# Layer-2 self-attention: the own block's mask enters the scores on TensorE instead of VectorE

## The chip, the cores and the metric

The kernel runs on one core of a Trainium2 chip. The metric is the device time of one execution in microseconds. A core has five engines that run their own instruction queues and meet at semaphores: TensorE (PE; its weight loads are listed as PEld), VectorE (DVE), ScalarE (ACT), GpSimd (POOL) and SyncE (SP), which here only issues DMAs. TensorE writes its products into PSUM, eight banks of 512 float32 columns on 128 partitions; VectorE and ScalarE read them there.

## The reference

The program is a decoder of four layers on x of shape (4, 512, 256) in float32. The change touches one of its twelve parts, the self-attention of layer 2:

```python
q = (x @ Wq.T + bq).reshape(B, T, H, D)      # B 4, T 512, H 16 heads, D 16
k = (x @ Wk.T + bk).reshape(B, T, H, D)
v = (x @ Wv.T + bv).reshape(B, T, H, D)
scores = jnp.einsum('bqhd,bkhd->bhqk', q, k) * attn_scale[0]
mask = _chunk_mask(T, CHUNK)                 # chunks of 64
scores = jnp.where(mask[None, None], -jnp.inf, scores)
attn = jax.nn.softmax(scores, axis=-1)
out = jnp.einsum('bhqk,bkhd->bqhd', attn, v).reshape(B, T, C)
return out @ Wo.T + bo
```

A query sees all keys of later chunks, none of earlier ones, and in its own chunk the keys up to itself. In tiles of 128 queries this means: the key tile of the same index (the own block) is partly masked, later tiles are whole, earlier ones drop out. The input of this part is the layer norm of the running x, and its result is added to x.

## The kernel before, in words

Each part of the model is a stage with its own block of five engine programs; a barrier stands between stages. `l2_attn` (from line 1691) is this stage. Its programs are unrolled lists in a fixed order, with waits on semaphores written out by hand; there is no planner.

**Items.** For each of 4 batches and each of 4 head groups (4 heads of 32 padded rows each, so that the four heads lie on the four 32-row strips of TensorE) there are 4 query tiles of 128: 64 items. An item has two score products. `score` (L1886) makes the scores with queries on the partitions, 128 x 512, 384, 256 or 128 key columns per head, only so that their row maximum can be taken. `row_max` on VectorE adds the mask to the own block, in PSUM, two heads at a time (L2101), and takes the negative maximum over each row, two heads at a time (L2105). When all four tiles of a group are through, the maxima are turned (unit "max") and added to the queries (L2075). `score_T` (L1899), seven items later, makes the scores again with the keys on the partitions, the maximum already in them; ScalarE takes the exponential (L1962), GpSimd cuts the masked part to zero (L2008, L2011), and `attend` (L1913) multiplies with the values and with a column of ones that gives the sums.

**Slots.** All engines walk through the same 79 slots. In slot n TensorE does `score(n)`, the units of `between(n)` (a key projection, a value projection, a turn of x, or the output product of the batch before), in every fourth slot `attend`, then `score_T(n - 7)`, and the units of `behind(n)` (a query projection, turning the maxima, picking and spreading the sums). Within a group the tiles come in the order 0, 3, 2, 1, so the scores have 512, 128, 256 and 384 columns per head.

**Banks.** The two score products share six banks, three pairs in turn (`pair_banks`); banks 6 and 7 serve the units. An item's four heads take two pairs. `pair_emptied` lets TensorE write a pair only after its last reader is done: VectorE's maximum (`maxed`) for `score`, ScalarE's exponential (`exped`) for `score_T`. In a slot, `score_T` needs the pair that the first maximum of that slot's `score` reads, and the next `score` needs the pair of the second maximum and that of the first exponential. `scored` is raised once per item, by the last of its four products.

**Loads.** SyncE loads the padded key and query weights first (`keys_loaded`), then mask, value weights, row vectors, the matrix that picks the sums, and the output weights (`loaded`). TensorE waits for `loaded` after the second score; VectorE waits for it before its first item. The mask is a 128 x 128 tile of 0 and -1e30. `k.ident`, the identity, is in place from the start of the program.

Of the kernel before, what the change touches and what calls it, by code (L numbers as in the profile page):

```python
# [16 lines left out]
ALU = mybir.AluOpType  # L17
# [3 lines left out]
P = 128  # L21
# [10 lines left out]
@contextmanager  # L32
def signals(nc, *names):

    with ExitStack() as st:
        sems = [st.enter_context(nc.semaphore(n)) for n in names]
        yield sems
        nums = sorted(s.num for s in sems)
        for n in nums:
            if n - 1 not in nums:  # L40
                last = n
                while last + 1 in nums:
                    last += 1
                nc.gpsimd.sem_clear(range(n, last + 1))
        nc.all_engine_barrier()
# [1645 lines left out]
def l2_attn(k):  # L1691
    nc = k.nc
    GR, HG, W = 4, 4, 512
# [6 lines left out]
    with ExitStack() as st:  # L1700
        wk, wq, wv, wo = (k.weight(n, st) for n in ("L2_padded_Wk", "L2_padded_Wq", "L2_attn_Wv", "L2_padded_Wo"))
        block_mask = k.const("block_mask", st)
# [19 lines left out]
        ps = k.ps  # L1722
# [40 lines left out]
        def score_op(n):  # L1763
            return n + max(0, n - AHEAD)
# [12 lines left out]
        def pair_banks(o, j):  # L1777
            first = 2 * ((2 * o + j) % 3)
            return slice(first, first + 2)

        with signals(nc, "keys_loaded", "loaded", "ones_set", "stats", "aggr", "shift", "rstd", "normed", "x_turned",
                     "x_moved", "k_projected", "k_made", "q_projected", "q_made", "v_projected", "v_half", "v_made") as (
                keys_loaded, loaded, ones_set, stats, aggr, shift, rstd, normed, x_turned, x_moved, k_projected, k_made,
                q_projected, q_made, v_projected, v_half, v_made), signals(
                nc, "scored", "masked", "maxed", "max_turned", "max_added", "scored_T", "exped", "cut_late", "cut",
                "attended", "summed_out", "picked_out", "inverse_copied", "spread_out", "inverted", "shared", "biased", "out_made", "out_added") as (
                scored, masked, maxed, max_turned, max_added, scored_T, exped, cut_late, cut, attended, sums_copied,
                sums_picked, inverse_copied, sums_spread, inverted, shared, biased, out_made, out_added), nc.Block() as block:

            @block.sync  # L1790
# [7 lines left out]
            LOADS = 16 * (4 + len(k.stage_rows))  # L1798

            @block.tensor  # L1800
            def _(pe):

                def unit(kind, b, i, bank):
                    if kind == "turn":
                        pe.wait_ge(normed, TT * (b + 1))
                        for t in range(TT):
                            last = pe.transpose(ps[:, bank, t * P:(t + 1) * P], xr[:, t, i * P:(i + 1) * P],
                                                k.ident[:, :])
                        last.then_inc(x_turned, 1)
                    elif kind in ("key", "query"):  # L1810
                        pe.wait_ge(x_moved, KC * (b + 1))
                        w = wk if kind == "key" else wq
                        for c in range(KC):
                            last = pe.matmul(ps[:, bank, :], w[:, c, i * P:(i + 1) * P], xT[:, c, :], start=c == 0,
                                             stop=c == KC - 1)
                        last.then_inc(k_projected if kind == "key" else q_projected, 1)
                    elif kind == "value":
                        for t in (2 * i, 2 * i + 1):
                            for c in range(KC):
                                last = pe.matmul(ps[:, bank, t % 2 * D:(t % 2 + 1) * D], xT[:, c, t * P:(t + 1) * P],  # L1820
                                                 wv[:, c, :], start=c == 0, stop=c == KC - 1)
                        last.then_inc(v_projected, 1)
                    elif kind == "max":
                        pe.wait_ge(maxed, 8 * i + 8)
                        for t in range(TT):
                            last = pe.transpose(ps[:, bank, t * P:(t + 1) * P],
                                                top[:, t, i % GR * P:(i % GR + 1) * P], k.ident[:, :])
                        last.then_inc(max_turned, 1)
                    elif kind == "pick":
                        pe.wait_ge(sums_copied, i + 1)  # L1830
                        for t in range(TT):
                            last = pe.matmul(ps[:, bank, HG * t:HG * t + HG], ou[:, i % 2, t * P:(t + 1) * P], sum_rows,
                                             start=True, stop=True)
                        last.then_inc(sums_picked, 1)
                    elif kind == "spread":
                        pe.wait_ge(inverse_copied, i + 1)
                        for t in range(TT):
                            last = pe.transpose(ps[:, bank, t * P:(t + 1) * P], wide[:, t * P:(t + 1) * P],
                                                k.ident[:, :])
                        last.then_inc(sums_spread, 1)  # L1840
                    else:
                        pe.wait_ge(shared, GR * (b + 1))
                        for t in (2 * i, 2 * i + 1):
                            for g in range(GR):
                                last = pe.matmul(ps[:, bank, t % 2 * D:(t % 2 + 1) * D],
                                                 oT[:, b % 2, g, t * P:(t + 1) * P], wo[:, g, :], start=g == 0,
                                                 stop=g == GR - 1)
                        last.then_inc(out_made, 1)
# [28 lines left out]
                def score(n):  # L1877
                    b, g, t, o = n // PER, n % PER // TT, TILE[n % TT], score_op(n)
                    if n % TT == 0:
                        pe.wait_ge(k_made, GR * b + g + 1)  # L1880
                        pe.wait_ge(q_made, GR * b + g + 1)
                    for j in range(2):
                        pair_emptied(o, j)
                    for h in range(HG):
                        r = slice(32 * h, 32 * h + 32)
                        last = pe.matmul(ps[:, pair_banks(o, h // 2).start + h % 2, 0:T - t * P],  # L1886
                                         qT[r, b % 2, g, t * P:(t + 1) * P], kT[r, b % 2, g, t * P:T], start=True,
                                         stop=True)
                    last.then_inc(scored, 1)

                def score_T(m):
# [30 lines left out]
                pe.wait_ge(keys_loaded, 32)  # L1922
                unit("key", 0, 0, 5)
                unit("query", 0, 0, 4)
                for n in range(SLOTS):
                    if n < ITEMS:
                        score(n)
                    if n == 1:
                        pe.wait_ge(loaded, LOADS)
                    for kind, b, i, bank in between(n):  # L1930
                        emptied(*before[bank])
                        unit(kind, b, i, bank)
                        before[bank] = (kind, b, i)
                    if attend_at(n) is not None:
                        emptied(*before[6])
                        attend(attend_at(n))
                        before[6] = ("attend", 0, attend_at(n))
                    if score_T_at(n) is not None:
                        score_T(score_T_at(n))
                    for kind, b, i, bank in behind(n):  # L1940
                        emptied(*before[bank])
                        unit(kind, b, i, bank)
                        before[bank] = (kind, b, i)
# [87 lines left out]
            def _(dve):  # L2031
# [62 lines left out]
                def row_max(n):  # L2094
                    b, g, t, o = n // PER, n % PER // TT, TILE[n % TT], score_op(n)
                    dve.wait_ge(scored, n + 1)
                    if b and n % TT == 0:
                        dve.wait_ge(max_turned, GR * (b - 1) + g + 1)
                    for j in range(2):
                        banks = pair_banks(o, j)  # L2100
                        dve.tensor_tensor(ps[:, banks, 0:P], ps[:, banks, 0:P],  # L2101
                                          block_mask[:, :].unsqueeze(1).to_broadcast([P, 2, P]),
                                          ALU.add).then_inc(masked, 1)
                        dve.wait_ge(masked, 2 * n + j + 1)
                        dve.tensor_reduce(  # L2105
                            top[:, t, g * P:(g + 1) * P].rearrange("p (h d) -> p h d", d=32)[
                                :, 2 * j:2 * j + 2, 16:17],
                            ps[:, banks, 0:T - t * P], AX.X, ALU.max, negate=True).then_inc(maxed, 1)
# [2861 lines left out]
```

## Time and profile before

| | |
|---|---|
| three timed runs | 3913.72, 3920.9, 3924.44 us; median 3920.9 |
| the profiled execution | 3895.01 us, span 3893.3 us |
| TensorE, share of the span | 89% |
| VectorE | 56% |
| ScalarE | 39% |
| GpSimd | 36% |
| mean granted TensorE clock | 0.932 of full |
| layer-2 self-attention | first score at 1586.53 us, last output product ends at 1944.51 us |

The page gives busy time per engine; an engine that is not busy waits for another, and what ended each wait is named behind the arrow in a row. Busy shares over the whole span mix twelve stages, so the rows below look at the one stage. A granted clock of 1.00 stands for 2.4 GHz and 0.50 for 1.2 GHz; a value between is the mean of stretches at either.

### The profile page before, as it was taken

Reading aid. Unit: us, or ns where it says so; the run is one execution under the profiler, and the core shown is the slowest. Engines: PE = TensorE matmul, PEld = TensorE weight load, DVE = VectorE, ACT = ScalarE, POOL = GpSimd, SP = SyncE. Lnnn points to the kernel's source line nnn. Section 1 sums busy time; section 2 is a strip of 40 time slices with the busy share of each in tenths; the row PEclk is TensorE's granted clock in tenths of the full one; section 3 lists DMA queues with packets and bytes.
Section 4 is the critical chain, followed back from the end, with each engine's and each line's share of the span. In section 5 each row is a group of like instructions: output and inputs, shape, how many; then the busy total and the mean of one; then the engine's idle time right before and its main releaser. Section 6 shows DMA issues by size and latency. Waiting matters only on the chain. (4 is left out here: it accounts for less than half of the span.)

```text
span 3893.3 us, 54516 instructions
## 1 busy us (share of the span) xinstructions
PE 3471.5 (89%) x18930; PEld 2243.6 (58%) x18930; DVE 2192.1 (56%) x5349; ACT 1506.5 (39%) x3064; POOL 1392.1 (36%) x1928
## 2 busy tenths in 40 slices
PE   7998897999999978788888999999896979997996
PEld 5675684445555557344444555556794445555996
DVE  6374444646555558666367676765434456665454
ACT  2253102434434265133344444443453134443453
POOL 2141441423223245233244445443423134443412
PEclk9999978999999988899889999999898889997998
DMA  2005001000000000000010000000421000003312
GB/s 101 1 1 125 15 1 46 1 1 1 1 1 1 13 1 1 24 1 1 1 49 1 1 1 1 1 1 1 165 90 60 1 29 1 1 1 112 126 57 83
DMA packets 48720, 108.86 MB, mean 28 GB/s; under 512 B 6660, under 2 KB 32900, under 8 KB 46404
## 3 DMA queue, kind: packets, MB, share of 16 engines
q1 hardware_dynamic: 40964, 84.88, 6.6%
q0 software_dynamic: 7488, 20.49, 1.5%
q8 instruction: 158, 2.59, 0.3%
q14 instruction: 110, 0.90, 0.1%
HBM read 70.67 MB, written 34.68 MB: 27 GB/s over the span
## 5 line engine op out<-in xcount | busy, mean ns | idle before, releaser
L2655 POOL TENSOR_SCALAR probs<-probs,inv_sum 128x512 f32<-128x512 f32 x640 | 438.2, 698 | 997.2 <-DVE inv_sum L2776 996.9
L2618 ACT ACTIVATE probs<-psum_banks,neg_max 128x576 f32<-128x576 f32 x640 | 468.5, 737 | 733.2 <-DVE neg_max L2861 733.2
L2861 DVE TENSOR_REDUCE neg_max<-psum_banks 128x1 f32<-128x576 f32 x640 | 455.0, 752 | 209.4 <-PE psum_banks L2493 202.8
L2493 PE MATMUL psum_banks<-keys_T,queries_T 64*128 64x288 f32 x2560 | 405.7, 436 | 52.5 <-ACT probs L2618 43.2
L2785 DVE COPY probs_T<-psum_banks 128x512 f32<-128x512 f32 x640 | 409.0, 680 | 4.2 <-PE psum_banks L2411 4.2
L2493 PEld LDWEIGHTS psum_banks<-keys_T,queries_T 64*128 64x128 f32 x2560 | 223.8, 189 | 268.8 <-ACT probs L2618 147.7
L2411 PE MATMUL psum_banks<-ident,probs 128*128 128x128 f32 x2560 | 357.6, 284 | 3.3 <-POOL probs L2655 2.4
L2411 PEld LDWEIGHTS psum_banks<-ident,probs 128*128 128x128 f32 x2560 | 281.2, 143 | 129.2 <-POOL probs L2655 75.2
L2443 PE MATMUL psum_banks<-probs_T,values 128*64 128x512 f32 x1280 | 311.3, 608 | 2.2 <-issue 2.2
L4419 PE MATMUL psum_banks<-sorted_T,tile_weights 128*128 128x128 f32 x2208 | 266.9, 278 | 0.0
L4419 PEld LDWEIGHTS psum_banks<-sorted_T,tile_weights 128*128 128x128 f32 x2208 | 259.5, 195 | 0.1
L2857 DVE TENSOR_TENSOR psum_banks<-psum_banks,key_mask 128x128 f32<-128x128 f32 x192 | 57.5, 299 | 273.3 <-PE psum_banks L2493 273.3
L2667 POOL TENSOR_TENSOR square_sum<-square_sum,neg_half 128x8 f32<-128x8 f32 x102 | 167.0, 1639 | 69.8 <-DVE square_sum L2751 68.3
L4318 POOL DMA_INDIRECT expert_outputs<-expert_rows,output_index x92 | 89.7, 975 | 268.6 <-DVE expert_rows L4703 115.8
L4435 PE MATMUL psum_banks<-w_L_experts_down,hidden_T 128*128 x736 | 174.3, 380 | 2.2 <-DVE expert_rows L4703 1.4
L2346 PE MATMUL psum_banks<-w_L_xattn_Wkv,batch_normed_T 128*128 128x512 f32 x320 | 156.3, 612 | 0.0
L2443 PEld LDWEIGHTS psum_banks<-probs_T,values 128*64 128x64 f32 x1280 | 78.9, 137 | 134.0 <-issue 123.2
L4500 ACT COPY tile_weights<-w_L_experts_up 128x1024 f32 (+1 forms) x92 | 135.3, 1472 | 22.9 <-issue 22.9
L4435 PEld LDWEIGHTS psum_banks<-w_L_experts_down,hidden_T 128*128 128x128 f32 x736 | 132.8, 190 | 17.2 <-issue 2.9
L1962 ACT ACTIVATE probs_T<-psum_banks 128x512 f32<-128x512 f32 (+3 forms) x128 | 83.0, 701 | 127.4 <-PE psum_banks L1899 126.5
L2658 POOL TENSOR_TENSOR context_probs<-probs,inv_sum 128x128 f32<-128x128 f32 x320 | 128.7, 402 | 0.0
L2618 ACT ACTIVATION_READ_ACCUMULATOR probs<-psum_banks,neg_max 128x1 f32 x640 | 125.4, 196 | 0.0
(538 smaller groups left out, 6160.1 us busy)
## 6 DMA issues: line engine op xcount, KB each, us to landing
normed<-sorted_rows SPq DMA_DIRECT2D x30, 385.5 KB, 3.4
sorted_rows<-zero_rows SPq DMA_DIRECT2D x8, 1028.0 KB, 16.6
w_L_experts_down<-in_L_experts_down SPq DMA_DIRECT2D x2, 4096.0 KB, 20.4
normed<-expert_outputs SPq DMA_DIRECT2D x8, 1024.0 KB, 6.9
w_L_xattn_Wkv<-in_L_xattn_Wkv SPq DMA_DIRECT2D x2, 2048.0 KB, 8.3
w_L_experts_up<-in_L_experts_up SPq DMA_DIRECT2D x1, 4096.0 KB, 12.2
sorted_rows<-zero_rows SPq DMA_DIRECT2D x4, 899.5 KB, 15.9
x_res<-in_x SPq DMA_DIRECT2D x4, 512.0 KB, 6.7
```

Of the source, the lines that this page charges most:

```text
L2346: last = pe.matmul(k.ps[:, 7, :], rows, wkv[:, c, W + a * 512:W + (a + 1) * 512], start=c == 0, stop=c == KC - 1)
L2411: last = pe.transpose(k.ps[:, 4 + n % 2, c * P:(c + 1) * P], prob[:, (b * NS + s) % PB, at + c * P:at + (c + 1) * P], k.ident[:, :])
L2443: last = pe.matmul(k.ps[r, 6, :], values[:, b % VB, c, (2 * j + h) * 64:(2 * j + h + 1) * 64], pT[:, q % 2, h, c, :], start=c == 0, stop=F ...
L2493: last = pe.matmul(k.ps[:, 2 * h + a, 0:HALF], qT[r, b % 2, j, t * P:(t + 1) * P], kT[r, j, k0:k0 + HALF], start=True, stop=True)
L2618: act.activation(prob[:, g % PB, h * w:(h + 1) * w].rearrange("p (a n) -> p a n", a=2), k.ps[:, 2 * h:2 * h + 2, 0:HALF], ACT.Exp, bias=nm ...
L2655: pool.tensor_scalar(w, w, inv[:, g % 4, h:h + 1], 1.0, ALU.mult, ALU.mult).then_inc(shared, 1)
L2667: pool.tensor_tensor(ss[:, i % 4, 2, :], ss[:, i % 4, 1, :], k.half[:, 0:8], ALU.pow).then_inc(inverted, 1)
L2785: dve.tensor_copy(pT[:, q % 2, h, :, t * P:(t + 1) * P], k.ps[:, 4 + n % 2, :].rearrange("p (c q) -> p c q", q=P)).then_inc(copied, 1)
L2861: dve.tensor_reduce(nmax[:, g % 4, h:h + 1], k.ps[:, 2 * h:2 * h + 2, 0:HALF], AX.XY, ALU.max, negate=True).then_inc(maxed, 1)
L4419: last = pe.matmul(ps[:, 2 * (n % 2) + part, f * P:(f + 1) * P], wt[:, n % 2, c, part * 512 + f * P:part * 512 + (f + 1) * P], xsT[:, n % ...
L4435: last = pe.matmul(ps[:, 6, 0:D], h[:, n % 2, f * P:(f + 1) * P], w_down[:, f // F, f % F * D:f % F * D + (E - 1) * STEP + D][:, bass.ds(a ...
L4500: act.copy(wt[:, n % 2, :, :], w_up[:, :, 0:(E - 1) * STEP + UP][:, :, bass.ds(at, UP)]).then_inc(weights_copied, 1)
```

## The change

The four score products of an item no longer close their accumulation. Four more products follow, one per head, each of the identity with the mask, which add the mask to the own block's 128 columns in PSUM; the last of these raises `scored`. VectorE's two additions per item and their semaphore `masked` are gone. TensorE's wait for the mask and the other late loads moves ahead of the first score.

```diff
--- before.py
+++ after.py
@@ -1782,9 +1782,9 @@
                      "x_moved", "k_projected", "k_made", "q_projected", "q_made", "v_projected", "v_half", "v_made") as (
                 keys_loaded, loaded, ones_set, stats, aggr, shift, rstd, normed, x_turned, x_moved, k_projected, k_made,
                 q_projected, q_made, v_projected, v_half, v_made), signals(
-                nc, "scored", "masked", "maxed", "max_turned", "max_added", "scored_T", "exped", "cut_late", "cut",
+                nc, "scored", "maxed", "max_turned", "max_added", "scored_T", "exped", "cut_late", "cut",
                 "attended", "summed_out", "picked_out", "inverse_copied", "spread_out", "inverted", "shared", "biased", "out_made", "out_added") as (
-                scored, masked, maxed, max_turned, max_added, scored_T, exped, cut_late, cut, attended, sums_copied,
+                scored, maxed, max_turned, max_added, scored_T, exped, cut_late, cut, attended, sums_copied,
                 sums_picked, inverse_copied, sums_spread, inverted, shared, biased, out_made, out_added), nc.Block() as block:
 
             @block.sync
@@ -1885,7 +1885,10 @@
                         r = slice(32 * h, 32 * h + 32)
                         last = pe.matmul(ps[:, pair_banks(o, h // 2).start + h % 2, 0:T - t * P],
                                          qT[r, b % 2, g, t * P:(t + 1) * P], kT[r, b % 2, g, t * P:T], start=True,
-                                         stop=True)
+                                         stop=False)
+                    for h in range(HG):
+                        last = pe.matmul(ps[:, pair_banks(o, h // 2).start + h % 2, 0:P], k.ident[:, :],
+                                         block_mask[:, :], start=False, stop=True)
                     last.then_inc(scored, 1)
 
                 def score_T(m):
@@ -1922,11 +1925,10 @@
                 pe.wait_ge(keys_loaded, 32)
                 unit("key", 0, 0, 5)
                 unit("query", 0, 0, 4)
+                pe.wait_ge(loaded, LOADS)
                 for n in range(SLOTS):
                     if n < ITEMS:
                         score(n)
-                    if n == 1:
-                        pe.wait_ge(loaded, LOADS)
                     for kind, b, i, bank in between(n):
                         emptied(*before[bank])
                         unit(kind, b, i, bank)
@@ -2098,10 +2100,6 @@
                         dve.wait_ge(max_turned, GR * (b - 1) + g + 1)
                     for j in range(2):
                         banks = pair_banks(o, j)
-                        dve.tensor_tensor(ps[:, banks, 0:P], ps[:, banks, 0:P],
-                                          block_mask[:, :].unsqueeze(1).to_broadcast([P, 2, P]),
-                                          ALU.add).then_inc(masked, 1)
-                        dve.wait_ge(masked, 2 * n + j + 1)
                         dve.tensor_reduce(
                             top[:, t, g * P:(g + 1) * P].rearrange("p (h d) -> p h d", d=32)[
                                 :, 2 * j:2 * j + 2, 16:17],
```

## Rows read from the trace of the kernel before

**Rows 1.** The page's busy times, and its 40 slices of 97 us.

```profile
PE 3471.5 (89%) x18930; PEld 2243.6 (58%) x18930; DVE 2192.1 (56%) x5349; ACT 1506.5 (39%) x3064; POOL 1392.1 (36%) x1928
...
PE   7998897999999978788888999999896979997996
```

**Rows 2.** Groups by line, 1580 to 1960 us: busy, mean ns, idle before, releasers.

```profile
L2105 DVE TENSOR_REDUCE neg_max<-psum_banks 128x2 f32<-128x1024 f32 (+3 forms) x128 | 105.7, 826 | 4.4
...
L1899 PE MATMUL psum_banks<-queries_below_max_T,keys_T 32*128 32x384 f32 (+3 forms) x512 | 59.1, 532 | 24.5 <-DVE neg_max L2105 22.0 <-ACT probs_T L1962 2.4
L1886 PE MATMUL psum_banks<-keys_T,queries_T 32*128 32x384 f32 (+3 forms) x512 | 55.6, 504 | 18.3 <-ACT probs_T L1962 8.8 <-DVE neg_max L2105 8.4 <-DVE queries_T L2054 1.0
L2101 DVE TENSOR_TENSOR psum_banks<-psum_banks,w_block_mask 128x256 f32<-128x256 f32 x128 | 54.6, 426 | 39.3 <-PE psum_banks L1886 39.3
```

**Rows 3.** By stretch (a head group each): length, PE, PEld, DVE, ACT, POOL busy, clock, DMA.

```profile
1586.53:1599.00 12.47, 9.03 (x48) 4.12 (x49) 10.94 (x22) 0.69 (x1) 0.00 (x0) 0.97 0.01 1
1599.00:1615.60 16.60, 13.00 (x60) 5.85 (x61) 14.21 (x30) 1.43 (x3) 4.02 (x7) 0.81 0.00 0
...
1653.97:1672.84 18.87, 16.60 (x129) 8.08 (x128) 14.21 (x30) 6.97 (x12) 5.51 (x17) 1.00 0.00 1
1672.84:1693.38 20.54, 18.27 (x129) 8.57 (x128) 13.90 (x26) 6.97 (x12) 9.57 (x23) 0.92 0.01 1
...
1716.93:1739.16 22.23, 19.96 (x137) 9.97 (x136) 12.68 (x21) 6.97 (x12) 5.50 (x17) 0.92 0.01 1
...
1802.94:1823.54 20.60, 18.33 (x138) 9.60 (x137) 12.63 (x21) 6.98 (x12) 5.52 (x17) 1.00 0.01 2
1823.54:1843.82 20.28, 18.17 (x129) 8.57 (x128) 12.60 (x22) 6.97 (x12) 5.50 (x17) 0.92 0.00 1
1843.82:1862.69 18.87, 16.60 (x129) 8.08 (x129) 12.60 (x22) 6.98 (x12) 8.25 (x21) 1.00 0.00 1
...
1883.28:1907.16 23.88, 19.05 (x130) 10.89 (x129) 11.92 (x20) 6.40 (x11) 5.51 (x17) 0.71 0.00 1
```

**Rows 4.** TensorE in order of time, one group: start, length, idle before.

```profile
1658.53 0.50 PE L1886 MATMUL psum_banks<-keys_T,queries_T 32*128 32x128 f32 x8 [0.41 <-DVE neg_max L2105]
1660.14 1.14 PE L1899 MATMUL psum_banks<-queries_below_max_T,keys_T 32*128 32x512 f32 x8 [1.11 <-DVE neg_max L2105]
...
1664.00 1.99 PE L1820 MATMUL psum_banks<-w_L_attn_Wv,batch_normed_T 128*128 128x256 f32 x8
1665.92 0.93 PE L1899 MATMUL psum_banks<-queries_below_max_T,keys_T 32*128 32x384 f32 x8
...
1667.87 0.93 PE L1886 MATMUL psum_banks<-keys_T,queries_T 32*128 32x384 f32 x8 [0.44 <-ACT probs_T L1962]
1668.73 2.36 PE L1913 MATMUL psum_banks<-probs_T,values_and_ones 128*32 128x512 f32 x32
...
1671.89 1.02 PE L1832 MATMUL psum_banks<-w_spread_sums,attended_sums_T 128*128 128x4 f32 x8 [0.15 <-ACT attended_sums_T L1984]
```

**Rows 5.** VectorE in order of time, second slot of that group.

```profile
1659.10 0.43 DVE L2101 TENSOR_TENSOR psum_banks<-psum_banks,w_block_mask 128x256 f32<-128x256 f32 x1 [0.63 <-PE psum_banks L1886]
1659.57 0.43 DVE L2105 TENSOR_REDUCE neg_max<-psum_banks 128x2 f32<-128x256 f32 x1
```

**Rows 6.** Order of time, 1559.5 to 1563 us: identity products of another stage.

```profile
1559.37 3.21 PEld L3508 LDWEIGHTS psum_banks<-ident,pair_weights 128*128 128x128 f32 x28
```

**Rows 7.** TensorE in order of time, a group with a low clock.

```profile
1745.32 2.09 PE L1899 MATMUL psum_banks<-queries_below_max_T,keys_T 32*128 32x512 f32 x8 [1.10 <-DVE neg_max L2105]
```

**Rows 8.** SyncE's last load of the stage, in order of time.

```profile
1569.53 0.53 SPq L1796 DMA_DIRECT2D w_L_padded_Wo<-in_L_padded_Wo  x1
```

**Rows 9.** DMA issues, 1560 to 1600 us: KB each, median us to landing.

```profile
w_L_padded_Wo<-in_L_padded_Wo SPq DMA_DIRECT2D x1, 512.0 KB, 5.7
```

**Rows 10.** TensorE in order of time, start of the stage.

```profile
1586.53 1.14 PE L1886 MATMUL psum_banks<-keys_T,queries_T 32*128 32x512 f32 x8 [1.00 <-DVE queries_T L2054]
```

## The prediction

> **What bounds the kernel now.** I read the page's busy shares first, then the sum by line for layer-2 self-attention alone, then the stage cut at the start of each group's first score, then TensorE and VectorE instruction by instruction in one group.
>
> TensorE is busy 89% of the span, and in the slices 16 to 20, where this stage lies, it shows 7 and 8 tenths [rows 1]. In the stage the added mask costs VectorE 54.6 us in 128 instructions, and the row maximum behind it 105.7 us [rows 2]. Together they are most of VectorE's work here, but VectorE doesn't set the pace: in a group of 18.87 us at full clock TensorE is busy 16.60 us and VectorE 14.21 or 12.60 us [rows 3]. Only the first two groups look different: in them VectorE is busy 10.94 of 12.47 us and 14.21 of 16.60 us, TensorE 9.03 and 13.00 [rows 3], because nothing of the second score product (L1899) is there yet.
>
> So from the third group on TensorE's own queue is the bound, with short gaps. In the group from 1653.97 there are four: 0.41 us before the 128-column score (VectorE's maximum of the slot before), 1.11 us before the 512-column transposed score (VectorE's maximum of this slot), 0.44 us behind ScalarE's exponential, and 0.15 us behind ScalarE's copy [rows 4]. Over the stage the waits for VectorE's maximum are 22.0 us before L1899 and 8.4 us before L1886 [rows 2]. That is all that relief of VectorE can give back in waits.
>
> **What the change does, part by part.** *Removed.* Per item (64 of them: 4 batches, 4 head groups, 4 query tiles) two additions of 0.43 us. Start to start from the addition to its reduction it is 0.47 us (1659.10 to 1659.57) [rows 5]; I use 0.46, so VectorE loses 128 x 0.46 = 58.9 us. It is worth something only where TensorE waits for it.
>
> *Added.* Per item four float32 products of 128x128 by 128x128. A plain float32 product stands as two instructions in the trace: the value unit is four products and shows 8 [rows 4]. So 8 more matmuls per item, 512 in all, each with its weight load. Their pace is that of the closest row, an identity product of the same shape: 28 loads take 3.21 us, so (3.21 - 0.19) / 27 = 0.112 us from one to the next [rows 6]. 8 x 0.112 = 0.90 us per item, 57.6 us in all. From above: the 8 instructions that pick the sums (4 columns each, nothing but weight loads) take 1.02 us [rows 4], 65 us for 64. From below: the attention product runs 32 instructions of 320 columns' mean in 2.36 us, 0.074 us each, since four heads share the array [rows 4]; the added products fill all 128 rows and columns and can't do that, so I take 0.90 and keep 0.59 as the low end.
>
> *Where it lies.* The four slots of a group, from [rows 4, 5]:
> - Slot 1 (512 columns): the key unit follows at once, so TensorE is 0.90 later. VectorE starts 0.90 later but saves 0.46 twice, so its maximum ends as before (0.90 - 0.92 = 0). The 0.41 us gap ahead of slot 2 is eaten: 0.90 - 0.41 = +0.49.
> - Slot 2 (128 columns): nothing lies between the score and the transposed score, which waits for the first maximum. The maximum starts 0.90 later and without the 0.46 of the addition: +0.44. The gap shrinks from 1.11 to 0.65 us.
> - Slot 3 (256 columns): the value unit stands behind, TensorE never waited: +0.90.
> - Slot 4 (384 columns): the score waits for the exponential, which is itself later by as much, so the 0.44 stays; the attention product stands behind: +0.90. The 0.15 gap also stays.
>
> Sum 2.73 us a group. Groups 3 to 16 are 14: 38.2 us. In the first two, VectorE's relief of 4 x 0.92 = 3.7 us a group meets 3.6 us of added TensorE time; TensorE then has 9.03 + 3.6 = 12.6 us of work in the first, which took 12.47, and 13.0 + 3.6 = 16.6 in the second, which took 16.60 [rows 3]. I take +1 each, between 0 and +3.6. Together +40.
>
> *The array's mode.* A switch from the heads' 32-row products to a full product shows already: the value unit starts its 8 instructions of 256 columns at 1664.00 and L1899 starts at 1665.92, 1.92 us for what streams in 8 x 0.213 = 1.71 (the pace from the scores: 1.14 us with 512 columns, 0.50 with 128, each head's two instructions in turn beside the other heads', so 0.64 / 6 = 0.107 per 128 columns) [rows 4]: 0.2 us a switch. In slots 1, 3 and 4 the switch was there before, only earlier; in slot 2 it is new and falls into the wait. I charge nothing. The Trainium skill (TensorEngine Tiling, Key Properties) says that a change of tiling mode drains TensorE; charged fully for slot 2 it would be 16 x 2 x 0.2 = 6 us more, and the trace agrees that a switch costs, but the wait covers it.
>
> *The clock.* Of the twelve groups from 1635.56 to 1883.28 seven have a granted clock of 0.92 or 0.93, the others 1.00 [rows 3]. Groups alike in work cost more for it: 20.54 against 18.87, 22.23 against 20.60 and 20.28 against 18.87 [rows 3], 1.4 to 1.7 us, some 10 us for seven. In the low ones TensorE goes from 2.4 to 1.2 GHz right at the 1.1 us gap: the 512-column product takes 2.09 us there instead of 1.14 [rows 4, 7]. The change fills a third to all of the two gaps before it, so I expect most of these stretches to go: -10 us. Equal gaps were passed at full clock in other groups, so this is no certainty; kept ends 0 and -15 (some of the last groups' stretches as well, clock 0.71 from 1883.28 [rows 3]). The Trainium skill (TensorE: Matmul & The Clock Gate, HAM oscillation) would have the clock fall only behind much longer idle gaps than these; by that rule the change gives nothing back and the sum is +40. The trace doesn't agree with the rule here.
>
> *Moved.* TensorE's wait for the weights stands before the first score instead of behind the second. The last load is issued at 1569.53 and lands 5.7 us later, at 1575.2 [rows 8, 9]; the first score starts at 1586.53, having waited for VectorE's queries [rows 10]. 11 us of cover, cost 0. Behind that wait the whole queue of TensorE would stand, but it is over by then.
>
> **Sum.** +38.2 + 2 - 10 = +30 us. The profiled execution took 3895.0 us (span 3893.3 and 1.7 around it) and would become 3925. The median of the runs shown is 3920.9, 25.9 above the profiled one; a difference within one stage should carry over, so 3951 us.
>
> **Rivals.** (a) The clock gives nothing back: all as above without the -10, +40, 3961 us. For it: at equal gaps the clock has stayed up and fallen, so gaps alone don't decide it. Against: in the seven groups it fell at these gaps.
> (b) TensorE pays in full: nothing is eaten, since the products themselves delay what VectorE would release, and the clock gives nothing: 64 x 0.90 = 58 us, 3979 us (65 and 3986 with the dearer row). For it: TensorE is the bound. Against: 1.52 us of each group are visible waits for VectorE.
> (c) On the other side, VectorE's relief decides. All waits for the maximum go (22.0 + 8.4), the clock returns 10, and the first two groups, VectorE-bound, gain 8 x 0.92 = 7.4 instead of paying; if the added products overlap like the attention ones, the other 56 items pay 56 x 0.59 = 33.0. Sum 33.0 - 30.4 - 10 - 7.4 = -15 us, 3906 us. It decides from a price below (30.4 + 10 + 7.4) / 56 = 0.85 us an item if every wait goes, but slot 2's wait can't go whole, since the products lie within it; so it needs both the low pace and that. The row of identity products speaks against it.
> (d) A wash: slot 2 and the starts absorb more than I count and the clock returns 15 or more: within 12 us of before, say +8, 3929 us.
>
> **How the numbers follow.** Forecast 0.50, (a) 0.20, (b) 0.11, (c) 0.05, (d) 0.14. A measurement of this kernel can tell about 0.3% from no change, 11.8 us. Faster: (c), 0.04. Same: (d) with the rest of (c), 0.13. Slower: 0.83. The range reaches from 3932 (+11, the pace of 0.107 that the 256-column stream would give, the clock at -15) to 3982 (the full price at 0.90 and a little); it also holds a few us of clock stretches in later stages, which may fall otherwise when everything there starts later.
>
> **What would show it.** Right: 512 instructions with the identity and the mask at 0.11 us each; a steady group at full clock of 21.6 us instead of 18.87; the gap before the 128-column score gone, that before the 512-column one 0.6 to 0.7 us, the 0.44 and 0.15 unchanged; clock 1.00 in most groups; VectorE at 59 us less in the stage and idle behind the scores. Wrong: groups of 18 to 19 us (then VectorE was the bound), or groups of 22.5 us and more (full price, or drains that I didn't charge); seven low groups as before (rival a); TensorE waiting before the first score.

## The result, and the profile after

The changed kernel takes 3939.16 us, median of 5 runs (3933.76 to 3946.76), against 3920.9 (3913.72 to 3924.44). The ratio is 1.0048, interval 1.0033 to 1.0063: slower by 18 us, 13 to 25. The forecast was 3951 us, slower, range 3932 to 3982.

The two profiled executions lie further apart, 3939.16 and 3895.01 us. Of these 44 us the stage holds 24: from its first score to its last output product 358.0 us before (1586.53 to 1944.51) and 382.1 us after. The other 20 lie in other stages, whose code is the same; the profiled execution of before was 26 us below its own median. It is the odd one: from the stage's last output product to the end of the span it took 1948.8 us, where the changed kernel and the seven experiments took 1965.5 to 1973.7. So the medians measure the whole, and the traces are read within the stage alone.

Busy times of the page after (they answer to [rows 1]):

```profile
PE 3519.2 (89%) x19442; PEld 2299.7 (58%) x19442; DVE 2135.9 (54%) x5221; ACT 1506.3 (38%) x3064; POOL 1393.2 (35%) x1928
```

The stage by line (as [rows 2]; line numbers have moved, L1902 is `score_T`, L2103 the maximum, L1890 the mask product):

```profile
L2103 DVE TENSOR_REDUCE neg_max<-psum_banks 128x2 f32<-128x1024 f32 (+3 forms) x128 | 99.6, 821 | 105.9 <-PE psum_banks L1890 105.9
...
L1890 PE MATMUL psum_banks<-w_block_mask,ident 128*128 128x128 f32 x512 | 74.1, 288 | 0.0
L1890 PEld LDWEIGHTS psum_banks<-w_block_mask,ident 128*128 128x128 f32 x512 | 61.9, 191 | 28.1 <-issue 26.2
L1902 PE MATMUL psum_banks<-queries_below_max_T,keys_T 32*128 32x384 f32 (+3 forms) x512 | 55.2, 500 | 14.8 <-DVE neg_max L2103 12.4 <-ACT probs_T L1964 2.4
...
L1886 PE MATMUL psum_banks<-keys_T,queries_T 32*128 32x384 f32 (+3 forms) x512 | 52.6, 478 | 12.4 <-ACT probs_T L1964 8.8 <-DVE neg_max L2103 1.1 <-DVE queries_T L2056 1.0
```

512 mask instructions have come to TensorE, 74.1 us busy, with as many weight loads, 61.9 us or 0.97 an item, and VectorE's additions with their 54.6 us are gone (its busy time in the stage fell from 208.94 to 155.85 us). TensorE's waits for the maximum fell from 22.0 to 12.4 us ahead of `score_T` and from 8.4 to 1.1 us ahead of `score`. VectorE now waits 105.9 us, for the mask product: it is ready long before its work is.

The stage cut at the first score of each head group (as [rows 3]: length, busy PE, PEld, DVE, ACT, POOL, granted clock). The last stretch is the last group with the tail of the stage.

```profile
1585.31:1599.05 13.74, 12.60 (x81) 7.72 (x81) 8.28 (x15) 0.69 (x1) 0.00 (x0) 1.00 0.01 1
1599.05:1614.73 15.68, 13.74 (x92) 8.55 (x93) 10.58 (x21) 1.43 (x3) 4.02 (x7) 1.00 0.00 1
1614.73:1636.13 21.40, 19.06 (x157) 10.83 (x157) 7.72 (x10) 7.84 (x13) 5.77 (x18) 1.00 0.00 1
...
1657.08:1678.83 21.75, 20.43 (x162) 11.80 (x161) 10.92 (x22) 6.98 (x12) 5.50 (x17) 1.00 0.00 1
...
1839.72:1861.47 21.75, 20.43 (x161) 11.80 (x160) 9.33 (x14) 6.97 (x12) 5.50 (x17) 1.00 0.00 1
...
1906.70:1967.38 60.68, 49.47 (x345) 29.23 (x344) 12.66 (x20) 18.57 (x30) 16.21 (x47) 0.80 0.00 1
sum 382.07, PE 348.73 PEld 205.89 DVE 155.85 ACT 114.56 POOL 102.71; mean PE 21.80 PEld 12.87 DVE 9.74 ACT 7.16 POOL 6.42
```

A group whose units are a key, a query and a value projection, as the one from 1657.08, takes 21.75 us instead of 18.87 at full clock, and the clock is at 1.00 in all fifteen groups before the last; before, seven of the twelve in the middle were below.

TensorE in one such group (answers to [rows 4]):

```profile
1658.15 1.16 PE L1890 MATMUL psum_banks<-w_block_mask,ident 128*128 128x128 f32 x8
1659.14 1.88 PE L1814 MATMUL psum_banks<-batch_normed_T,w_L_padded_Wk 128*128 128x512 f32 x4
...
1662.17 0.50 PE L1886 MATMUL psum_banks<-keys_T,queries_T 32*128 32x128 f32 x8
...
1664.37 1.14 PE L1902 MATMUL psum_banks<-queries_below_max_T,keys_T 32*128 32x512 f32 x8 [0.61 <-DVE neg_max L2103]
1665.44 1.98 PE L1814 MATMUL psum_banks<-batch_normed_T,w_L_padded_Wq 128*128 128x512 f32 x4
...
1669.00 1.89 PE L1820 MATMUL psum_banks<-w_L_attn_Wv,batch_normed_T 128*128 128x256 f32 x8
1670.82 0.93 PE L1902 MATMUL psum_banks<-queries_below_max_T,keys_T 32*128 32x384 f32 x8
...
1672.77 0.93 PE L1886 MATMUL psum_banks<-keys_T,queries_T 32*128 32x384 f32 x8 [0.43 <-ACT probs_T L1964]
1673.63 1.16 PE L1890 MATMUL psum_banks<-w_block_mask,ident 128*128 128x128 f32 x8
1674.71 2.36 PE L1916 MATMUL psum_banks<-probs_T,values_and_ones 128*32 128x512 f32 x32
...
1677.87 1.03 PE L1832 MATMUL psum_banks<-w_spread_sums,attended_sums_T 128*128 128x4 f32 x8 [0.15 <-ACT attended_sums_T L1986]
```

The reader is to see the mask products, 8 instructions a slot (those of the second and third are left out here), that the next unit starts 0.99 us after they start (1658.15 to 1659.14) and the attention product 1.08 after (1673.63 to 1674.71), that the gap before the 128-column score (1662.17) is gone, that before the 512-column product (1664.37) is 0.61 instead of 1.11, and that 0.43 and 0.15 us behind ScalarE are as before.

### The profile page after: what moved, and what is told of

Read it like the earlier page. It is cut to its first block and busy times, and to the rows that moved or that the text cites. A ratio compares the mean times of both kernels' runs of the same rounds, so it can differ in the third digit from the quotient of the medians.

```text
span 3937.4 us, 55411 instructions
## 1 busy us (share of the span) xinstructions
PE 3519.2 (89%) x19442; PEld 2299.7 (58%) x19442; DVE 2135.9 (54%) x5221; ACT 1506.3 (38%) x3064; POOL 1393.2 (35%) x1928
## 5 line engine op out<-in xcount | busy, mean ns | idle before, releaser
L2103 DVE TENSOR_REDUCE neg_max<-psum_banks 128x2 f32<-128x1024 f32 (+3 forms) x128 | 99.6, 821 | 105.9 <-PE psum_banks L1890 105.9
```

## The experiments

All are timed against the kernel before: 3919.5 us in the first four (15 runs), 3921.3 in the last three (17 runs). For each the same cut of the stage was made. The first two and the kernels before and after make a square of four: mask on VectorE, on TensorE, on both, on neither.

**Both: the added products without the relief.** The changed kernel, and in `row_max`:

```diff
                         banks = pair_banks(o, j)
+                        dve.tensor_tensor(ps[:, banks, 0:P], ps[:, banks, 0:P],
+                                          block_mask[:, :].unsqueeze(1).to_broadcast([P, 2, P]),
+                                          ALU.add).then_inc(masked, 1)
+                        dve.wait_ge(masked, 2 * n + j + 1)
                         dve.tensor_reduce(
```

> The changed kernel with VectorE's two additions per item put back behind the mask products (the mask goes in twice, which leaves the maxima as they are). It shows the added products without the relief. Theory (TensorE's queue sets the pace, VectorE's relief is worth only the two waits ahead of slot 1's and 2's successors): a steady group of 22.7 to 22.9 us instead of 21.75, the gap before the 128-column score back at 0.4 and that before the 512-column one at 1.1 us; 3953 to 3957 us (14 groups x 1.0 and a few us in the first two more than the changed kernel's 3939). Rival (VectorE's relief is worth nothing, all the slots are TensorE's): 3939. Rival (VectorE's relief carries most, 58.9 us): over 3980.

Measured: 3965.1 us, ratio 1.012 (1.0104 to 1.0136). Groups by stretch (two of them, and the sum of the stage) and then TensorE in the first of these groups:

```profile
1664.61:1687.58 22.97, 20.57 (x162) 11.80 (x161) 14.30 (x30) 7.08 (x12) 5.49 (x17) 1.00 0.00 1
...
1760.80:1785.18 24.38, 22.14 (x161) 12.32 (x160) 14.30 (x30) 7.07 (x12) 5.47 (x17) 0.93 0.01 1
...
sum 405.99, PE 355.44 PEld 208.21 DVE 210.37 ACT 115.86 POOL 102.54; mean PE 22.22 PEld 13.01 DVE 13.15 ACT 7.24 POOL 6.41
```

```profile
1668.72 0.50 PE L1902 MATMUL psum_banks<-queries_below_max_T,keys_T 32*128 32x128 f32 x8 [0.16 <-DVE neg_max L2107]
...
1670.23 0.50 PE L1886 MATMUL psum_banks<-keys_T,queries_T 32*128 32x128 f32 x8 [0.42 <-DVE neg_max L2107]
...
1672.89 1.14 PE L1902 MATMUL psum_banks<-queries_below_max_T,keys_T 32*128 32x512 f32 x8 [1.08 <-DVE neg_max L2107]
1674.19 1.98 PE L1814 MATMUL psum_banks<-batch_normed_T,w_L_padded_Wq 128*128 128x512 f32 x4 [0.16 <-DVE attended_T L2088]
```

A group takes 22.97 us: the gaps of 0.42 and 1.08 us are back, as is the 0.16 ahead of the query unit, and there is one of 0.16 ahead of the 128-column `score_T`. So the relief is worth 22.97 - 21.75 = 1.22 us a group, all of it in slots 1 and 2, 24 us in the stage (406.0 to 382.1) and 26 in the medians. The total came out 8 us above the expectation: the relief was under-sized. The group makes up 0.2 us of it each time (1.22 for 1.0). The rest lies in four stretches: the third group (24.49 against 21.40 us, clock 0.93), the fourth (22.64 against 20.95), the one from 1760.80 (24.38, clock 0.93) and the last stretch (63.64 against 60.68). VectorE's relief is thus neither nothing nor its full 58.9 us.

**Neither: the relief without the products.** This kernel leaves the mask out of the row maximum; the maximum is then over more keys.

```diff
-                                         stop=False)
-                    for h in range(HG):
-                        last = pe.matmul(ps[:, pair_banks(o, h // 2).start + h % 2, 0:P], k.ident[:, :],
-                                         block_mask[:, :], start=False, stop=True)
+                                         stop=True)
```

> No mask in the first score product on any engine: the row maximum is then taken over some keys too many in the own block, which still is an upper bound to subtract before the exponential; the masked weights are cut to zero afterwards as before. It shows the relief without the added products. Theory: slot 1 gives 0.3, slot 2 0.46 and 0.2 us, 18.87 becomes 17.9 us a group at full clock: 14 us in 14 groups, some 5 in the first two, and the clock stays up (10 or more): 3890 to 3897 us. Rival (gaps still there, so the clock falls as before): 3901. Rival (VectorE off the path wholly): 3911 to 3921.

Measured: 3875.5 us, ratio 0.9893 (0.9877 to 0.9908). By stretch, and TensorE in the second slot:

```profile
1579.60:1589.61 10.01, 8.83 (x49) 4.08 (x49) 8.11 (x15) 0.69 (x1) 0.00 (x0) 1.00 0.01 2
1589.61:1601.56 11.95, 9.98 (x61) 4.91 (x61) 10.87 (x21) 1.43 (x3) 4.11 (x7) 0.99 0.00 0
...
1638.87:1656.68 17.81, 16.47 (x130) 8.08 (x129) 10.84 (x22) 6.98 (x12) 5.51 (x17) 1.00 0.00 1
...
1845.98:1899.79 53.81, 41.62 (x313) 24.98 (x312) 12.67 (x20) 18.57 (x30) 16.21 (x47) 0.87 0.01 1
sum 320.19, PE 285.19 PEld 146.72 DVE 154.87 ACT 114.70 POOL 102.83; mean PE 17.82 PEld 9.17 DVE 9.68 ACT 7.17 POOL 6.43
```

```profile
1644.20 1.14 PE L1899 MATMUL psum_banks<-queries_below_max_T,keys_T 32*128 32x512 f32 x8 [0.63 <-DVE neg_max L2100]
```

A group takes 17.81 us at full clock, 1.06 below the 18.87 of before (some 0.97 had been expected), and 21.75 - 17.81 = 3.94 us below the changed one, 0.985 us a slot. That is the price of four float32 mask products with nothing hidden, since TensorE's wait in slot 2 is the same in both (0.63 and 0.61 us). It isn't the same in every slot. From one 32-row score's start to the next the slots take 4.20, 4.12, 4.52 and 4.97 us here and 5.09, 5.19, 5.41 and 6.06 in the changed kernel: 0.89, 1.07, 0.89 and 1.09 us more. In slots 1 and 3 another full product follows at once; in slots 2 and 4 the mask products are the only full ones in their place. The total is 15 us below the lower end of the expectation. Two places hold most of it: the first two groups, in which VectorE sets the pace, went from 29.07 to 21.96 us, 7.1 and not 5, and the last stretch from 61.23 us at a clock of 0.75 to 53.81 at 0.87, 7.4 us that I had not counted.

**Filler: only the gap is filled.** The kernel before, and in TensorE's loop:

```diff
+                    if n < ITEMS and n % 4 == 1:
+                        emptied(*before[7])
+                        for h in range(HG):
+                            pe.matmul(ps[:, 7, h * P:(h + 1) * P], k.ident[:, :], block_mask[:, :], start=True,
+                                      stop=True)
```

> The kernel before with four products of the identity and the mask into an idle bank, ahead of the transposed score of every second slot of a group, that is inside the 1.1 us gap; their result is never read. It adds no work to the path and takes none away, only the gap in TensorE's activity is filled. Theory (the low clock stretches come from these gaps): granted clock 1.00 in all groups from 1635 on, like groups all at 18.9 and 20.6 us, and 10 us less: 3908 to 3912 us. Rival (the stretches have nothing to do with the gap): seven low groups as before, 3921. Rival (the filler delays the product behind it): groups longer by 0.1 to 0.9 us at full clock, 3921 to 3930.

Measured: 3906.3 us, ratio 0.9964 (0.9951 to 0.9978), 13 us faster by added work alone. By stretch:

```profile
1600.39:1615.55 15.16, 11.54 (x69) 6.04 (x69) 14.00 (x30) 1.43 (x3) 4.02 (x7) 0.91 0.01 2
...
1673.26:1692.12 18.86, 17.69 (x137) 9.05 (x136) 13.90 (x26) 6.97 (x12) 9.54 (x23) 1.00 0.01 2
...
1873.16:1934.50 61.34, 49.32 (x321) 28.88 (x320) 16.13 (x28) 18.56 (x30) 16.14 (x47) 0.78 0.00 1
sum 346.59, PE 310.22 PEld 165.06 DVE 208.66 ACT 114.50 POOL 102.55; mean PE 19.39 PEld 10.32 DVE 13.04 ACT 7.16 POOL 6.41
```

All twelve groups from 1635.98 to 1873.16 have a clock of 1.00. Groups that took 20.54 and 20.28 us [rows 3] take 18.86 or 18.87, and none is longer by more than 0.01 us than its like at full clock before. The gaps of 0.41 and 0.43 us in them are still there; only that of 1.1 us is filled. So the low stretches in these groups did come from the 1.1 us gap, and four unread products in it are enough to keep TensorE at 2.4 GHz. From the fifth group to the last stretch it is 218.8 us instead of 229.3 (from 1654.40 and from 1653.97), 10.5 us.

**Split: the signal raised per pair of heads.** The changed kernel with:

```diff
                                          block_mask[:, :], start=False, stop=True)
-                    last.then_inc(scored, 1)
+                        if h % 2:
+                            last.then_inc(scored, 1)
...
-                    dve.wait_ge(scored, n + 1)
...
                     for j in range(2):
+                        dve.wait_ge(scored, 2 * n + j + 1)
```

> The changed kernel with the signal raised twice per item: after the mask products of heads 0 and 1, and after those of heads 2 and 3; VectorE's first maximum starts on the first. Theory: only slot 2 of a group waits for the first maximum, so its gap goes from 0.61 to 0.15 us: 0.45 x 14 = 6 us, 3932 to 3934 us, nothing in the other slots. Rival (the wait in slot 2 then ends with something else, the exponential or the second pair): 3939.

Measured: 3924.9 us, ratio to before 1.0011 (1.0001 to 1.002), so 14 us below the changed kernel. TensorE in the second slot, and two stretches with the sum:

```profile
1660.13 1.16 PE L1890 MATMUL psum_banks<-w_block_mask,ident 128*128 128x128 f32 x8
1661.45 1.14 PE L1903 MATMUL psum_banks<-queries_below_max_T,keys_T 32*128 32x512 f32 x8 [0.16 <-DVE neg_max L2104]
```

```profile
1654.61:1675.91 21.30, 20.42 (x161) 11.80 (x161) 11.03 (x22) 6.97 (x12) 5.50 (x17) 1.00 0.01 1
...
1899.31:1953.08 53.77, 42.46 (x345) 26.99 (x344) 12.76 (x20) 18.57 (x30) 16.21 (x47) 0.97 0.01 1
sum 367.57, PE 341.70 PEld 203.65 DVE 157.65 ACT 114.60 POOL 102.72; mean PE 21.36 PEld 12.73 DVE 9.85 ACT 7.16 POOL 6.42
```

The gap is 0.16 us, the group 21.30 instead of 21.75, as the theory has it, and no other slot of such a group moved. But 14 us is more than 6. Eleven groups give 4.9, the first four 2.7, and the last stretch 6.9 (60.68 to 53.77 us): its clock is 0.97 here and 0.80 in the changed kernel. Whether the split brings that or the moment at which the tail begins was not tried.

**bfloat16 mask products.** The changed kernel with bfloat16 copies of the identity and the mask, made once by GpSimd; TensorE waits for them ahead of its loop (the allocation of the two tiles is left out):

```diff
-                        last = pe.matmul(ps[:, pair_banks(o, h // 2).start + h % 2, 0:P], k.ident[:, :],
-                                         block_mask[:, :], start=False, stop=True)
+                        last = pe.matmul(ps[:, pair_banks(o, h // 2).start + h % 2, 0:P], ident16[:, :],
+                                         mask16[:, :], start=False, stop=True)
...
                 pe.wait_ge(loaded, LOADS)
+                pe.wait_ge(ones_set, 5)
...
+                pool.tensor_copy(ident16[:, :], k.ident[:, :]).then_inc(ones_set, 1)
+                pool.wait_ge(loaded, LOADS)
+                pool.tensor_copy(mask16[:, :], block_mask[:, :]).then_inc(ones_set, 1)
```

> The changed kernel with the identity and the mask copied once to bfloat16 tiles (two GpSimd copies before the first item), so that the four mask products of an item are bfloat16 with one instruction each instead of two; the scores stay float32. It shows whether the price is that of the instructions. Theory (price by TensorE's time): the mask part takes 0.3 to 0.45 us an item instead of 0.99, a steady group comes to 18.9 to 19.5 us instead of 21.75; 3898 to 3908 us. Rival (the price is the switch between the heads' 32-row products and the full ones, not their time): 0.8 us an item remain, 3928 to 3939.

Measured: 3894.6 us, ratio 0.9923 (0.991 to 0.9936). TensorE in slots 3 and 2 of two groups, and by stretch:

```profile
1676.46 0.40 PE L1892 MATMUL psum_banks<-block_mask,ident 128*128 128x128 bf16 x4
1676.69 1.95 PE L1822 MATMUL psum_banks<-w_L_attn_Wv,batch_normed_T 128*128 128x256 f32 x8
...
1690.64 0.40 PE L1892 MATMUL psum_banks<-block_mask,ident 128*128 128x128 bf16 x4
1691.65 1.14 PE L1904 MATMUL psum_banks<-queries_below_max_T,keys_T 32*128 32x512 f32 x8 [0.61 <-DVE neg_max L2109]
```

```profile
1648.18:1667.00 18.82, 17.50 (x145) 8.91 (x145) 10.94 (x22) 6.98 (x12) 5.51 (x17) 1.00 0.01 2
...
1865.80:1922.27 56.47, 44.31 (x329) 26.00 (x328) 12.67 (x20) 18.57 (x30) 16.22 (x47) 0.85 0.00 1
sum 334.15, PE 300.01 PEld 159.23 DVE 156.01 ACT 114.57 POOL 102.73; mean PE 18.75 PEld 9.95 DVE 9.75 ACT 7.16 POOL 6.42
```

The next unit starts 0.23 us after the mask products start (1676.46 to 1676.69) instead of 0.99, and a group takes 18.82 us: 1.01 us above the one without any mask, 0.25 a slot against 0.985. So at least three quarters of the price were the time of the eight float32 instructions; the switch between the heads' strips and the full array, which is made as often here, can be no more than the 0.25 that is left. With this the same idea, mask on TensorE, beats the kernel before by 27 us with the same maxima.

**bfloat16 and split.** The edits of the last two together.

> As the bfloat16 one, and the signal is raised once per pair of heads. Theory: with cheap products only half of their time, 0.15 to 0.2 us, is left to gain in slot 2, 3 us in all, and slot 1's second maximum comes no earlier: 3895 to 3906 us. Rival (no gain, VectorE's maxima are no longer waited for): as the bfloat16 one.

Measured: 3897.9 us, ratio 0.9935 (0.9918 to 0.9952). By stretch:

```profile
1646.15:1664.86 18.71, 17.50 (x146) 8.91 (x145) 10.94 (x22) 6.98 (x12) 5.51 (x17) 1.00 0.01 2
...
1862.54:1927.00 64.46, 52.62 (x329) 30.33 (x328) 12.66 (x20) 18.57 (x30) 16.21 (x47) 0.71 0.00 1
```

A group takes 18.71 us, 0.11 less than 18.82; the gap in slot 2 is 0.50 us instead of 0.61. The medians don't show it: the last stretch ran at a clock of 0.71 and took 64.46 us instead of 56.47. What the split gives here is below what the clock of the tail takes or leaves.

**The moved wait alone.** The kernel before with `pe.wait_ge(loaded, LOADS)` ahead of the loop.

> The kernel before with only TensorE's wait for the late loads moved ahead of the first score. Theory: the loads are 11 us early, nothing changes: 3919 to 3922 us and the first score starts as before behind VectorE's queries. Rival (the wait holds the first score): a start later by the difference, 3925 or more.

Measured: 3922.8 us, ratio 0.9999 (0.9991 to 1.0008). The first score, and the sum of the stage:

```profile
1585.93 1.14 PE L1886 MATMUL psum_banks<-keys_T,queries_T 32*128 32x512 f32 x8 [1.00 <-DVE queries_T L2053]
```

```profile
sum 363.75, PE 312.22 PEld 154.26 DVE 209.03 ACT 114.69 POOL 102.86; mean PE 19.51 PEld 9.64 DVE 13.06 ACT 7.17 POOL 6.43
```

It is released by VectorE's queries, as in [rows 10]. The stage takes 363.75 us here and 357.98 in the profile of before, although only a wait that costs nothing differs. The low clock stretches fell otherwise: the third and fourth groups took 23.05 and 20.02 us at clocks of 0.79 and 0.91, where they had taken 19.96 and 18.41 at 0.92 and 1.00, and the last stretch 63.90 us at 0.71 for 61.23 at 0.75. 6 us of the stage are such play. This execution, of 3924.87 us, lies near the median of before, which the profiled one of before doesn't; against its stage the changed kernel's is 382.07 - 363.75 = 18.3 us longer, as much as the medians differ by.

## Why the prediction was right, step by step

**Direction and bound.** TensorE's queue sets the pace from the third group on. Right: what is added there is paid, 0.985 us a slot at full clock, and what is taken from VectorE comes back as 1.06 to 1.22 us of the 3.68 a group.

**The pace.** 0.112 us an instruction, 0.90 us an item, from identity products of another stage. The loads take 0.97 us for eight, (0.97 - 0.19) / 7 = 0.111 each; the pace is right. The price of a slot is 0.985 on average: 8 x 0.111 = 0.89 in slots 1 and 3, as the sum had it, and 1.07 and 1.09 in slots 2 and 4, where the products stand alone between others that use the array in strips. No experiment tells whether those 0.2 us are the two more switches or something else at the ends of such a run; the bfloat16 kernel's slots 2 and 4 cost 0.30 and 0.33 us against 0.19 in the others.

**The slots.** Predicted +0.49, +0.44, +0.90, +0.90, 2.73 in all. Measured, from one 32-row score's start to the next in the two groups at full clock: 5.09 for 4.56 (+0.53), 5.19 for 4.82 (+0.37), 5.41 for 4.52 (+0.89) and 6.06 for 4.97 (+1.09), 2.88 in all. Slot 2 came out near its figure by luck. `score_T` starts 2.20 us after the score (1662.17 to 1664.37) where it was 1.61 (1658.53 to 1660.14 [rows 4]), 0.59 later and not 0.44: what the mask products take beyond 0.90 isn't covered by the wait, as the prediction had it, but lengthens the slot, since VectorE's maximum, which ends the wait, starts only behind them. But the wait for `attended_T` behind it went as well, which I hadn't counted:

```profile
1661.44 1.98 PE L1814 MATMUL psum_banks<-batch_normed_T,w_L_padded_Wq 128*128 128x512 f32 x4 [0.16 <-DVE attended_T L2086]
```

That line is of before; in the changed kernel the query unit starts 1.07 us behind `score_T` (1664.37 to 1665.44) and not 1.30, which takes 0.23 back. In slots 1 and 3 the unit behind the mask products now follows full products on full products and is shorter for it, in slot 3 1.82 us from its start to `score_T`'s (1669.00 to 1670.82) where it was 1.92 [rows 4]; that hides a part of the 0.99. Slot 4 has no such unit and pays 1.08 from the mask to the attention product. So a charge of some 0.2 us was due in slots 2 and 4 each, whatever its cause, and none was made. From 1.92 less 1.82 I estimate the entry from strips into full products at 0.1 us. The Trainium skill's rule that a change of tiling mode drains TensorE (TensorEngine Tiling, Key Properties) agrees with this in kind.

**The early groups.** +2 for the first two; measured +0.35 against before (29.42 for 29.07), and +1.8 against the filler kernel (27.64), whose clock is higher there. Right within its bounds.

**The clock.** -10 us. The filler kernel gives 13 us in the medians and 11.4 in the stage (346.6 for 358.0; against the stage of the kernel with the moved wait it would be 17.2), and the changed kernel has a low clock only in its last stretch. The mechanism was right, and it decides the size: without it the same change costs 382.1 - 346.6 = 35.5 us in the stage. The rule that the clock falls only behind much longer idle gaps (the Trainium skill, TensorE: Matmul & The Clock Gate, HAM oscillation) would have given no return; no gap of the seven low groups is longer than 1.11 us, and filling it ended the low stretches, so the measurement decides against it here.

**The sum.** Predicted +30. The stage has +24.1: -11.4 for the clock, +1.8 for the first two groups, and +33.7 where I had 38.2. The difference is in the term of 14 equal groups: the eleven from the fifth on cost 30.9 (249.6 us for the filler's 218.8), near 11 x 2.73, and the fourth +2.5, but the third +1.0 and the last with its tail -0.7. The third group had a clock of 0.90 in the filler kernel and 1.00 in the changed one, and the last group of the filler kernel began low as well (its 512-column `score_T` took 2.03 us) and the changed one's did not: there the clock gave back part of the price, +0.4 for the last group (22.07 to 22.49 us), and the tail behind it was 1.1 us shorter, for which no run shows a cause. At equal clocks the third group isn't cheaper: it is 2.98 us longer in the changed kernel than in the bfloat16 one (21.40 and 18.42), a steady one 2.93. So the term that was too large is that of 14 groups paying 2.73 beside a return of the clock in the middle groups only. The medians, +18, lie another 6 lower, as much as the stage of before varies with its clock.

**The range.** Its lower end doesn't follow from the two terms named for it. At 0.107 us an instruction the slots give 0.45 + 0.40 + 0.86 + 0.86, 2.55 a group; 14 of these, 2 for the first groups and 15 of clock come to +23 us, and not to +11. The measured +18 lies below that. So the forecast's range held the result because it was drawn wider than its own terms; by them it would have missed.

**The rivals.** (a), no return of the clock, falls with the filler kernel. (b), full price, falls: with both masks, where nothing is relieved, the medians rise by 46 us with the clock returned, and the relief takes 26 of them back. The full price is there at nearly equal clock: the stage with both masks is 59.4 us longer than the filler's (406.0 and 346.6), near the rival's 58. (c) needed VectorE to decide and a pace of 0.074; the first holds only in the first two groups, the second nowhere in float32. Its condition on the price, below 0.85 us an item, is nevertheless met by the bfloat16 kernel: 0.25 us a slot, and it is faster. (d), a wash, fell short, though 18 us is nearer to its +8 than to +30.

## What to carry to other kernels

Moving an operation from an engine with time to spare to the engine that sets the pace costs its whole time there, and gives back only the waits that it shortens; read both from one period of the steady state, slot by slot. The square of both, one, the other and neither tells price and relief apart with two extra kernels: here 0.985 us a slot against 1.06 to 1.22 us a group. Before an operation is moved ask for its cheapest form, and whether it is needed: a mask in bfloat16 took a quarter of the time, and without it in the maximum the kernel takes 3875 us, the fastest of all. That last form subtracts a larger bound than needed and holds only while masked scores don't lie so far above the visible ones that their exponentials vanish.

## What the runs showed of the hardware

Four unread float32 products in a gap of 1.1 us, once in a group of about 20 us with TensorE 88% busy (16.60 of 18.87 us [rows 3]), made the kernel 13 us faster, ratio 0.9964 (0.9951 to 0.9978), because the granted clock stayed at 2.4 GHz. The length of a gap alone doesn't decide. With both masks and gaps of 0.42 and 1.08 us one of the twelve middle groups is low where the kernel before, with 0.41 and 1.11, had seven. In the changed kernel two gaps of 1.14 us in the first two groups (ahead of 1599.05 and 1613.22) and in the filler kernel one of 1.42 (ahead of 1647.49) brought no low stretch, while in the kernel without the mask the clock fell at one of 0.63 us (at 1850.79, a product of 2.09 us instead of 1.14), 1.6 us behind one of 1.44.

Four bfloat16 products of 128x128 by 128x128 into banks that hold float32 sums cost 0.25 us on average, four float32 ones 0.985 us.

The last stretch of the stage, its last group and the tail, took 53.8 to 64.5 us with nearly the same work, at clocks of 0.97 to 0.71 (56.5 and 64.5 us in the two bfloat16 kernels, whose work is the same). Differences of a few us between such kernels can't be read from medians alone.
